# Zone weights in other dead buffers, a later fold and finer router steps in a two-layer macaron kernel

## What is computed

```python
x = x + 0.5 * L0_ffn(layernorm(x))     # f0: 8 experts of 176, top 2, and a shared one of 352
x = x + L0_attn(layernorm(x))          # a0: 16 heads of 8
x = x + 0.5 * L0_ffn(layernorm(x))     # f0
x = x + 0.5 * L1_ffn(layernorm(x))     # f1: 8 zones, top 3 for each batch
x = x + L1_attn(layernorm(x))          # a1: latent attention, 8 heads
x = x + 0.5 * L1_ffn(layernorm(x))     # f1
```

```python
pooled = x.mean(axis=1)
probs = softmax(tanh(pooled @ W1 + b1) @ W2 + b2)
top_p, top_i = top_k(probs, 3); top_w = top_p / top_p.sum(-1)
out = x + sum over e of w[:, e] * (gelu(x @ Wa[e]) @ Wb[e])    # Wa: 128 x 512, Wb: 512 x 128
```

## Time and profile before

| | us |
|---|---|
| median of 3 runs | 1515.67 (1513.77 to 1516.41) |
| the profiled execution | 1514.86 |
| its span, first to last instruction | 1513.1 |
| PE busy | 1439.8 (95%), 9752 matmuls |
| DVE busy | 1120.1 (74%) |
| ACT busy | 975.6 (64%) |
| POOL busy | 595.6 (39%) |
| second f0, loop of tiles | about 665 to 911 |
| f0 to the first zone product | 911 to 943.2 |
| first f1 | 943.2 to about 1107 |

### The profile page before, as it was taken

One profiled execution on the slowest core, in us unless ns is written; L12 is line 12 of the kernel. 1 busy time (PEld: TensorE's weight loads), 2 busy tenths in 40 slices (PEclk: granted clock), 3 DMA queues, 4 the chain that ended last, 5 costly groups with the idle time before them and its releaser, 6 DMA issues.

```text
span 1513.1 us, 27605 instructions
## 1 busy us (share of the span) xinstructions
PE 1439.8 (95%) x9752; PEld 1158.4 (77%) x9752; DVE 1120.1 (74%) x2433; ACT 975.6 (64%) x1759; POOL 595.6 (39%) x580
## 2 busy tenths in 40 slices
PE   6999999979999999999999988999979999989998
PEld 6888887765666665688888766989967777769998
DVE  3776777688888888476777786687768888866765
ACT  6456555547777777755665645777736666667886
POOL 4466666630000000025666555667710111136664
PEclk9999999999999999999999998999999999999999
DMA  6000000000000000010000002000000000000001
GB/s 177 1 1 1 1 1 1 1 0 1 1 1 1 1 1 1 2 72 1 1 1 1 1 0 98 1 1 2 1 1 1 2 2 1 2 2 1 16 15 29
DMA packets 13321, 16.88 MB, mean 11 GB/s; under 512 B 768, under 2 KB 10496, under 8 KB 12928
## 3 DMA queue, kind: packets, MB, share of 16 engines
q1 hardware_dynamic: 13184, 15.11, 3.3%
HBM read 13.01 MB, written 2.10 MB: 10 GB/s over the span
## 4 chain that ended last, share of the span: by engine, by line
PE 77%; DVE 10%; ACT 5%; issue 4%; POOL 3%; DMA 1%; SPq 0%; DVEq 0%; POOLq 0%; ACTq 0%
PE PS L623 16%; PE PS L1732 8%; PE PS L651 8%; PE PS L1749 8%; PE PS L772 5%; PE PS L792 5%; PE PS L780 4%; PE PS L1156 2%; PE PS L751 2%; PE PS L1160 2%; PE PS L1131 2%; PE PS L170 2%; PE PS L1113 1%; PE PS L1141 1%; PE PS L1180 1%
## 5 line engine op out<-in xcount | busy, mean ns | idle before, releaser
L531 POOL TENSOR_TENSOR RR<-AR,RR 128x512 fp32r<-128x512 f32 x150 | 193.8, 1292 | 490.1 <-ACT RR L558 484.5
L501 DVE TENSOR_TENSOR AR<-AR,PS 128x512 f32<-128x512 f32 x224 | 153.1, 684 | 91.5 <-PE PS L623 83.5
L593 ACT ACTIVATE AR<-PS 128x512 f32<-128x512 f32 x224 | 132.8, 593 | 132.4 <-PE PS L623 130.4
L891 ACT ACTIVATE AR<-PS 128x512 f32<-128x512 f32 x256 | 152.3, 603 | 85.8 <-PE PS L780 85.1
L968 DVE TENSOR_REDUCE AR<-PS 128x2 f32<-128x512 f32 x256 | 172.3, 685 | 21.9 <-PE PS L772 21.2
L623 PE MATMUL PS<-XHI,WU 128*128 128x512 f32 x448 | 176.7, 394 | 6.9 <-DVE AR L501 6.7
L623 PE MATMUL PS<-XHI,WG 128*128 128x512 f32 x448 | 177.2, 396 | 0.3 <-ACT AR L593 0.3
L505 DVE TENSOR_TENSOR AR<-AR,PS 128x512 f32<-128x512 f32 x224 | 153.9, 687 | 8.0 <-POOL RR L531 0.3
L1826 ACT ACTIVATE PS<-PS 128x1024 f32<-128x1024 f32 x96 | 96.8, 1009 | 65.8 <-PE PS L1732 65.5
L1732 PE MATMUL PS<-XHI,SL 128*128 128x256 f32 x576 | 134.0, 288 | 1.9 <-DVE XTR L1893 1.9
L772 PE MATMUL PS<-XLO,XHI 128*128 128x512 f32 x256 | 130.4, 510 | 5.1 <-DVE XHI L961 2.7
(11 more groups left out here) (276 smaller groups left out, 3520.8 us busy)
## 6 DMA issues: line engine op xcount, KB each, us to landing
X<-in_x SPq DMA_DIRECT2D x4, 512.0 KB, 6.5
RAWZ<-in_zone_up SPq DMA_DIRECT2D x8, 256.0 KB, 3.9
RAWZ<-in_zone_down SPq DMA_DIRECT2D x8, 256.0 KB, 5.0
out_x<-X SPq DMA_DIRECT2D x4, 512.0 KB, 3.2
AR<-in_w SPq DMA_DIRECT2D x1, 1792.0 KB, 11.4
XT<-in_w SPq DMA_DIRECT2D x1, 1608.0 KB, 8.0
XT<-in_sel SPq DMA_DIRECT2D x1, 896.0 KB, 6.3
SM<-in_small SPq DMA_DIRECT2D x1, 857.5 KB, 7.2
```

What stands on the lines that cost most here:

```text
L501: v.tensor_tensor(PRD[:, m % 2, :], SIL[:, m % 2, :], bank(2 + m % 2), ALU.mult).then_inc(S.prod, 1)
L531: g.tensor_tensor(HL[k % 3], GAT[:, m % 2, :], HH[k % 3].bitcast(F32), ALU.subtract).then_inc(S.h_lo, 1)
L593: act.activation(SIL[:, m % 2, :], bank(m % 2), ACT.Silu).then_inc(S.silu, 1)
L891: act.activation(PT[:, g % 2, k, 2 * jp:2 * jp + 2, :], bank(2 + m % 2).rearrange("p (j q) -> p j q", j=2), ACT.Exp, scale=SC0).then_inc(S ...
```

## The change

- The load of the zones: slots 0, 1, 2 in AR as early as before, at other places; zones 6 and 7 go straight into the lower halves of their places in `ZW` (`RAWL`) once PE has spread the last weights of f0; zones 3, 4 behind the last gate, 5 behind the last low half. The order is `LOADS`.
- The splits: high halves in the order `HIGHS`, zones 0 and 6 ahead of the last accumulator copy; POOL subtracts 6, 2, 7 and DVE 0, 1, 3, 4, 5, the first of each at the end of f0.
- The fold: its outputs are made right behind the heads, in bank 6; ACT and DVE take the values behind the splits; the bias of it follows zone product 1 on PE and 0 on ACT, `prep_pool_late` follows POOL's first three selections, `prep_pool_early` runs at the end of a0's POOL program. One of two `keep_busy` runs and two waits of PE are gone.
- In every f0: the power at m = 7, the bias at m = 10, the normalising at m = 11 to 13.
- The router: a pick becomes two steps (`route_best`, `route_drop`), the weights two (`route_weights`, `route_diagonal`), and the tiles or z at which they stand change.

```diff
@@ -125,7 +125,7 @@
         SL = nc.alloc_sbuf_tensor_at("SL", [P, TOP1, 2, 2, FF1], F32R, offset=ar_at)
-        RAWZ = nc.alloc_sbuf_tensor_at("RAWZ", [P, 6, 2, FF1], F32, offset=ar_at)
+        RAWL = nc.alloc_sbuf_tensor_at("RAWL", [P, E1, 2, 2, FF1], F32, offset=experts_at)
@@ -182,8 +182,10 @@
-        POOL_LO = (0, 3, 6)
-        DVE_LO = (1, 2, 4, 5, 7)
+        HIGHS = (0, 6, 7, 1, 2, 3, 4, 5)
+        POOL_LO = (6, 2, 7)
+        DVE_LO = (0, 1, 3, 4, 5)
+        LOADS = (0, 1, 2, 6, 7, 3, 4, 5)
@@ -278,11 +280,11 @@
         ROUTE_A1 = names(dict(bank=bank(0), ready=FIRST, smax=NH1 * NB, tokens=0, tanh=0, hidden=2, logits=2, exp=3, softmax=3,
-                              picks=(3, 4, 5), weights=6, spread=7, known=7))
+                              picks=((3, 3), (4, 4), (5, 5)), weights=(6, 6), spread=7, known=7))
...
         ROUTE_F0 = names(dict(bank=bank(5), ready=FIRST // 2, smax=0, tokens=R0 + 5, tanh=R0 + 6, hidden=R0 + 7, logits=R0 + 8,
-                              exp=R0 + 9, softmax=R0 + 10, picks=(R0 + 11, R0 + 12, R0 + 13), weights=R0 + MT0,
-                              spread=R0 + MT0 + 2, known=R0 + MT0 + 4))
+                              exp=R0 + 10, softmax=R0 + 10, picks=((R0 + 11, R0 + 12), (R0 + 13, R0 + 14), (R0 + 15, R0 + 16)),
+                              weights=(R0 + 18, R0 + 19), spread=R0 + 20, known=R0 + 22))
@@ -505,7 +507,7 @@
                         back(c - 1)
-                    if ahead(n) and m == 9 and not first:
+                    if ahead(n) and m == 10 and not first:
@@ -516,6 +518,7 @@
                 next_low(NC - 2)
+                split_low(v, n + 1, DVE_LO[0], ST[n + 1].z_lo2)
@@ -530,11 +533,13 @@
                                     ALU.subtract).then_inc(S.h_lo, 1)
-                    if ahead(n) and m == 8 and c > 0:
+                    if ahead(n) and m == 7 and c > 0:
...
                 chunk(c)
+            if to_zones(n):
+                split_low(g, n + 1, POOL_LO[0], ST[n + 1].z_lo)
@@ -595,14 +600,20 @@
                         high(c - 1, MT0 - 1)
-                    if ahead(n) and 10 <= m < 10 + TPC and not first:
-                        next_normed(c - 1, m - 10)
+                    if ahead(n) and m > 10 and not first:
+                        next_normed(c - 1, m - 11)
+                    if ahead(n) and m == MT0 - 1 and not first:
+                        next_normed(c - 1, TPC - 1)
...
                 next_copy(NC - 2)
+            if to_zones(n):
+                act.wait_ge(S.u_pe, D.u_pe + tiles0)
+                for e in HIGHS[0:2]:
+                    split_high(n + 1, e)
@@ -726,6 +737,7 @@
                 g.tensor_tensor(xs, xs, T.bo.unsqueeze(1).to_broadcast([P, TPC, H]), ALU.add).then_inc(S.xb, 1)
+            prep_pool_early(stages.index("a1"))
@@ -1459,16 +1471,22 @@
             for h in range(NH1):
-                pe.matmul(bank(7)[0:1, 0:H], R.buv[:, h:h + 1], R.wo[:, h * H:(h + 1) * H], start=(h == 0), stop=False)
-            pe.matmul(bank(7)[0:1, 0:H], ones[0:1, 0:1], T.bo1[0:1, :], start=False, stop=True).then_inc(S.prep_pe, 1)
+                pe.matmul(bank(6)[0:1, 2 * H:3 * H], R.buv[:, h:h + 1], R.wo[:, h * H:(h + 1) * H], start=(h == 0), stop=False)
+            pe.matmul(bank(6)[0:1, 2 * H:3 * H], ones[0:1, 0:1], T.bo1[0:1, :], start=False, stop=True).then_inc(S.prep_pe, 1)
+
+        def prep_pe_bias(n):
+            S = ST[n]
+            pe = nc.tensor
             pe.wait_ge(S.prep_copy, 3)
-            pe.matmul(bank(7)[:, H:2 * H], ones[0:1, :], cb[0:1, :], start=True, stop=True).then_inc(S.prep_pe, 1)
+            pe.matmul(bank(6)[:, 3 * H:4 * H], ones[0:1, :], cb[0:1, :], start=True, stop=True).then_inc(S.prep_pe, 1)
...
             act.wait_ge(S.blank, 1)
+            act.wait_ge(ST[n - 1].z_lo, len(POOL_LO))
+            act.wait_ge(ST[n - 1].z_lo2, 2)
@@ -1477,9 +1495,13 @@
             act.activation(cg, bank(6)[:, 0:2 * H], ACT.Copy).then_inc(S.prep_copy, 1)
-            act.activation(cb[0:1, :], bank(7)[0:1, 0:H], ACT.Copy).then_inc(S.prep_copy, 1)
+            act.activation(cb[0:1, :], bank(6)[0:1, 2 * H:3 * H], ACT.Copy).then_inc(S.prep_copy, 1)
+
+        def prep_act_bias(n):
+            S = ST[n]
+            act = nc.scalar
             act.wait_ge(S.prep_pe, 3)
-            act.activation(CBB, bank(7)[:, H:2 * H], ACT.Copy).then_inc(S.prep_copy, 1)
+            act.activation(CBB, bank(6)[:, 3 * H:4 * H], ACT.Copy).then_inc(S.prep_copy, 1)
@@ -1492,8 +1514,7 @@
             g = nc.gpsimd
-            sem, count = x_done(n - 1)
-            g.wait_ge(sem, count)
+            g.wait_ge(ST[stages.index("a0")].xb, NC)
@@ -1506,6 +1527,7 @@
             g.wait_ge(S.blank, 2)
+            g.wait_ge(ST[n - 1].sel_d, TOP1)
@@ -1526,7 +1548,13 @@
         LATE = bank(4)[:, SEQ:2 * SEQ]
-        ZSLOT = (0, 5, 2, 3, 4, 1, 0, 5)
+        RAW_AT = (0, 5120, 6144, 1728, 2752, 3776)
+
+        def raw_zone(e):
+
+            if e < len(RAW_AT):
+                return ar(RAW_AT[e], 2 * FF1).rearrange("p (i f) -> p i f", i=2)
+            return RAWL[:, e, :, 1, :]
@@ -1537,24 +1565,23 @@
             sp.wait_ge(F.w_all, B.w_all + 1)
-            for e in range(E1):
-                z_in, before = zone_sems(n)[e % 4], D.z_in0 + e // 4 * 32
-                if e == 2:
-                    if n == PREP_IN:
-                        prep_sp(n + 1)
-                    sp.wait_ge(F.down, B.down + tiles0)
-                    if n == PREP_IN:
-                        prep_sp_out(n + 1)
+            if n == PREP_IN:
+                prep_sp(n + 1)
+            for i, e in enumerate(LOADS):
+                z_in = zone_sems(n)[i % 4]
+                if i >= 4:
+                    sp.wait_ge(z_in, 32)
+                if e == 6:
+                    sp.wait_ge(F.w_pe, B.w_pe + 2 * NC)
+                if e == 3:
+                    sp.wait_ge(F.gated, B.gated + tiles0)
                 if e == 5:
-                    sp.wait_ge(F.back, B.back + NC)
-                if e >= 4:
-                    sp.wait_ge(z_in, before)
-                if e == 6:
-                    sp.wait_ge(S.z_lo, D.z_lo + 1)
-                if e == 7:
-                    sp.wait_ge(S.z_lo2, D.z_lo2 + 1)
-                sp.dma_start(RAWZ[:, ZSLOT[e], 0, :], a.zone_up[e]).then_inc(z_in, 16)
-                sp.dma_start(RAWZ[:, ZSLOT[e], 1, :], a.zone_down[e]).then_inc(z_in, 16)
+                    sp.wait_ge(F.h_lo, B.h_lo + tiles0)
+                sp.dma_start(raw_zone(e)[:, 0, :], a.zone_up[e]).then_inc(z_in, 16)
+                sp.dma_start(raw_zone(e)[:, 1, :], a.zone_down[e]).then_inc(z_in, 16)
+            if n == PREP_IN:
+                sp.wait_ge(F.down, B.down + tiles0)
+                prep_sp_out(n + 1)
@@ -1579,14 +1606,14 @@
             act = nc.scalar
-            act.wait_ge(zone_sems(n)[e % 4], D.z_in0 + e // 4 * 32 + 32)
-            act.activation(ZW[:, e, :, 0, :], RAWZ[:, ZSLOT[e], :, :], ACT.Copy).then_inc(S.z_hi, 1)
+            i = LOADS.index(e)
+            act.wait_ge(zone_sems(n)[i % 4], i // 4 * 32 + 32)
+            act.activation(ZW[:, e, :, 0, :], raw_zone(e), ACT.Copy).then_inc(S.z_hi, 1)
...
             S, D = ST[n], counts(n)
-            eng.wait_ge(S.z_hi, D.z_hi + e + 1)
-            eng.tensor_tensor(ZW[:, e, :, 1, :], RAWZ[:, ZSLOT[e], :, :], ZW[:, e, :, 0, :].bitcast(F32),
-                              ALU.subtract).then_inc(sem, 1)
+            eng.wait_ge(S.z_hi, D.z_hi + HIGHS.index(e) + 1)
+            eng.tensor_tensor(ZW[:, e, :, 1, :], raw_zone(e), ZW[:, e, :, 0, :].bitcast(F32), ALU.subtract).then_inc(sem, 1)
@@ -1631,11 +1658,16 @@
-        def route_pick(v, n, k, rows):
+        def route_best(v, n, k, rows):
             ch, r = route_chain(v, n), slice(0, rows)
-            tv, ti = TOPV[r, k:k + 1], TOPI[r, k:k + 1]
+            tv = TOPV[r, k:k + 1]
...
             ch.link(v.scalar_tensor_tensor(EQR[r], LR[r], tv, rev[r], ALU.is_equal, ALU.mult))
+            route_end(ch)
+
+        def route_drop(v, n, k, rows):
+            ch, r = route_chain(v, n), slice(0, rows)
+            ti = TOPI[r, k:k + 1]
@@ -1648,11 +1680,14 @@
             ch.link(v.tensor_scalar(TOPI[r], TOPI[r], -1.0, float(E1), ALU.mult, ALU.add))
+            route_end(ch)
+
+        def route_diagonal(v, n, rows):
+            r = slice(0, rows)
...
             last.then_inc(ST[n].r_dve, 1)
-            route_end(ch)
@@ -1691,10 +1726,14 @@
             for k in range(TOP1):
-                if m == at.picks[k]:
-                    route_pick(v, n, k, FIRST)
-            if m == at.weights:
+                if m == at.picks[k][0]:
+                    route_best(v, n, k, FIRST)
+                if m == at.picks[k][1]:
+                    route_drop(v, n, k, FIRST)
+            if m == at.weights[0]:
                 route_weights(v, n, FIRST)
+            if m == at.weights[1]:
+                route_diagonal(v, n, FIRST)
@@ -1705,13 +1744,8 @@
```

(48 more changed lines are left out.)

## The result

The changed kernel takes 1492.66 us (median, 1491.13 to 1494.61) against 1516.04 us in the same comparison: ratio 0.9846, interval 0.9831 to 0.9861. That is 23.4 us less; 23.7 were forecast. Measured once more beside the last experiments it was 1489.43 against 1514.64 us, ratio 0.9832 (0.9818 to 0.9845). Its first profiled execution took 1493.59 us, with a span of 1491.8. It is the execution whose rows are shown. Lines have moved in the new source: L501 is L503, L623 is L634, L651 is L662, L1583 is L1611, L1588 is L1616, L1732 is L1766.

A forecast was written before the change was run, and what follows sets the result against it. The prediction took TensorE (PE), busy 95% of the span, to bound the kernel. Gains of 6.8 + 7.3 + 8.4 + 1.2 = 23.7 us from a median of 1515.67 gave 1492.0 us, range 1486 to 1502.

The forecast's parts named there:

- A: Layernorm's steps in f0: PE's wait at m = 12 goes, 0.57 us in each of 12 chunks, 6.8 us gained.
- C: From f0 to the zones: earlier loads, splits and fold, fewer fillers, start the zones sooner; 8.4 us gained, bounds 4 and 12.
- B: Router in chunks 6 and 7 of the second f0: finer steps remove PE's waits; 7.3 us gained, bounds 4 and 7.7.
- D: Late picks in both f1 stages, z = 16 to 22: 1.2 us gained, bounds -1 and 2.5.
- the spare that the prediction gave it: f0 loop: DVE has some 0.6 us to spare per tile, and PE needs its product only two tiles later.
- PE asks for that silu two tiles later, 3.4 us: Router's exp in f0: ACT's table loads and exp take about 2.8 us, PE needs the silu after 3.4 us.
- The router's own products: Second f0: PE's three router products stay, at not more than 0.43 us each, say 1.1 us in all.
- the half level until the fillers: Way to the zones: PE's clock at 1.2 GHz, outputs 6.8 us, transposes 1.1, fillers 4.5 us.
- rival 1: Way to the zones: the fold's outputs bring full clock, C is 12 in place of 8.4, 1488.4 us; chance 0.17.
- 0 to 1.5 us of wait: Both f1 stages: cost at the spread of moving the weights from z = 21 to 22, twice.
- Rival 2: f0: PE waits for silus delayed by ACT's XN copies and exp; 17.1 us gained in all, 1498.6 us; chance 0.17.
- Rivals 3 and 4: 3: in-place zone loads do nothing, 1499.9 us, chance 0.06. 4: POOL's power delays all 14 chunks, 1518.7 us, chance 0.04.

The follow-up runs named there:

- e12: The changed kernel itself measured again, unaltered, beside the last experiments: 1489.43 us.
- e8: The changed kernel with POOL's power moved back to m = 8, the bias still at m = 10: 1491.98 us.
- e1: The changed kernel with the layernorm's steps undone in both f0 (power m = 8, bias m = 9, normalising m = 10 to 13): 1498.59 us.
- e9: The changed kernel with the early router's softmax at tile 11 and each pick one tile later: 1490.77 us.
- e3: The kernel before with only the layernorm's steps, the f0 router's steps and the late picks changed; the way to the zones as before: 1502.59 us.
- e2: The changed kernel with the router in the second f0 back at its old tiles, the layernorm's steps as changed: 1496.79 us.
- e11: The changed kernel with zones 0 and 6's high halves behind the last accumulator copy and DVE's first low half behind its last back addition: 1493.27 us.
- e4: The changed kernel with the late picks, weights and diagonal of both f1 stages at their old steps: 1490.50 us.
- e5: The changed kernel without the twelve filling products ahead of the first zone product: 1492.41 us.
- e6: The changed kernel with the late weights and diagonal at z = 21 in both f1 stages, picks as changed: 1491.31 us.
- e7: The changed kernel with DVE subtracting seven low halves and POOL only zone 6: 1487.98 us.
- e10: The changed kernel with the alterations of e4, e7 and e9 together: 1486.48 us.

## Why the prediction was right

The time is 0.7 us from the forecast, but the terms were not all right. The mechanisms of A and C are the ones described. A and C gained 0.6 and 2.0 us more than forecast, B and D 1.2 and 1.7 less, so that the sum came out is luck. It also depends on the comparison: the same kernel measured again (e12) was 25.2 us faster than the one before, not 23.4.

**A, 6.8 us forecast.** Right in mechanism and size. The chunks went from 30.56 to 29.96 us, 0.60 each and not 0.57, since the tile behind the wait also loses 0.03: 4.38 us in the first f0, 3.0 in chunks 1 to 5 of the second, 7.4 in all. The tail of the first f0, 0.5 us, comes with it and was in no term. The power's move was needless: e8 shows that the later bias, with the normalising behind it, does it alone. That DVE may be late by some 1.7 us there (0.48 and 1.25 in e8) and PE still does not wait fits the spare that the prediction gave it.

**B, 7.3 us forecast, 6.1 found** (9.07 less 3.0). The step that failed is "PE asks for that silu two tiles later, 3.4 us", taken as enough. PE did not wait for the silu, but DVE stood 2.32 us for it and then had bias, softmax and a held instruction of 1.30 us in the same tile; PE paid for that at tile 13. The bias was there by A's own move, and I had priced the two parts apart: e1, with the bias at m = 9, and e9, with the softmax at tile 11, both lose this wait and shorten chunk 6 by 0.9 us. I had named the spread as the one wait over 0.3 us; PE does not wait there, since the diagonals, apart from POOL now, took 0.31 us. The router's own products were also put too low: even in e9, where the only wait is one of 0.55 us at the spread, the loop is 2.3 us longer than that of the first f0, which has no router (238.55 against 236.26), so the products cost some 1.7 us, where I had 1.1.

**C, 8.4 us forecast, 10.4 found** (9.86 and the tail's 0.50, counted here as the prediction did; but e3, with the old way, has the shorter tail too, 6.76 us, and e1 has not, so the tail comes with A's steps. By e3 the way alone is 10.4.) The chain is the one described: ACT's high halves without a gap, the low halves ending 12.9 us behind the last transposes where the forecast had 12.0 (928.4 less 916.4), PE deciding in the end. The mis-sized term is the clock. I had the half level until the fillers, 6.8 us for the outputs and 4.5 for the fillers; they took 5.5 and 2.8 us. Against that the heads, where the clock fell sooner, took 0.9 us more than forecast. It is a case between forecast and rival 1, and e1 and e2 price rival 1: with a clock that holds through the outputs the way is 15.1 us, 1.3 us less, which makes C 11.7 us. So the 12 us of rival 1 were nearly right, and the 8.4 of the forecast were too few. With full clock PE waits for POOL's selection, which I had 1 us too early. e3 undoes the way as a whole and e11 the early splits alone (2.35 us); how the rest is shared between the loads, the order and the fold is not shown. What the heads do to the clock differs from profile to profile: in the changed kernel's first PE was busy in all of 908 to 926, and the clock fell in both profiles of the changed kernel and in e4, e5, e6, e8 and e9, while in e1, e2, e7, e10 and e11 it held. A forecast should hold both cases. The Trainium skill, "TensorE: Matmul & The Clock Gate", Part 1, has the gate follow PE's busyness; by it alone I would have had the clock hold in all of them, so these rows bear it out in part only.

**D, 1.2 us forecast, -0.5 found.** The step that failed is the "0 to 1.5 us of wait" at the spread, taken near its lower end: the wait is 1.35 us in the first f1, as large as the one that was removed, with 0.49 us more at an up product, and e6 shows it is DVE's work in one place or the other. In the second f1 neither is seen, and I should not have counted a gain there: the waits in it, near z = 16 to 21, are the same before and after.

**Not in the sum:** the loss of 3 us at the start, the 1.0 us between the two f0, whose cause is open, and 1.4 us behind the first zone product (77.33 less the 75.94 of e4), of which D takes 0.5 and the ledger shows the other 0.9. The first and the last go with the clock's level, as the rows under the ledger and under e3 show.

**The rivals.** Rival 2 (ACT in f0) is half true in one tile. Of its other half, ACT's two copies at m = 13, PE shows nothing. Rivals 3 and 4 are out: zones 6 and 7 were there in time (ACT took zone 6 at 904.70 without a wait), and PE shows no wait for POOL within the loops. The Trainium skill, "ScalarE: Activation LUTs", section "What ACT_TABLE_LOAD costs", has about 2.66 us for a switch; the row has a silu at 864.53 behind a load of 1.28 us at 863.24. By that page my estimate was that PE stands about 2 us there; PE does not wait at that silu, and the row shows no drain behind the load.

## What to carry to other kernels

An engine that asks for a value before it can be there pays for it downstream, in the tile where its own consumer runs out of slack: here moving the question was enough. Look first at what already stands in the tile to which it moves. Before sharing bulk two-input subtractions between DVE and POOL, add up what each takes alone: here the elapsed time was about that sum, so every one given to the engine that needs 1.2 us instead of 2.34 (POOL at 911.42 in the changed kernel) shortens the whole, as e7 shows. Where the critical engine's clock may or may not hold, price both cases, and compare kernels by stretches between fixed landmarks, since a median of a few runs mixes the clock's luck with the change.

## What the runs showed of the hardware that I had not expected

- The start, which is the same in all these kernels on PE, ended between 52.75 and 58.89 us (first gate product). In the changed kernel's first profile it was late with the half level between 20 and 30 us; in e2, the latest, the granted clock was 1.00, 0.90, 0.93 and 0.66 in the four stretches of 10 us from 20 on. That is about as much clock lost in all as in the changed kernel's first profile, and e2 began 2.8 us later, so the clock is not the whole cause and the rest is open.
- DVE and POOL took turns on these two-input instructions: five subtractions on DVE took 5.8 us alone (e7), three took 5.64 us beside POOL. Even a 128x4 instruction (`next_bias`) is held, 0.16 us alone and 2.30 beside one of POOL's zone subtractions.
- A gapless PE can be at either level in the same products: the heads of e1 and e7 kept a granted clock of 1.00; in the changed kernel's first profile it was 1.00 in 908 to 910, 0.65 in 910 to 912 and 0.50 in 912 to 916, with PE busy in all of it.
